# Another order at the seam between two matmul stages: tile 7's copy and W's scale ahead of ar's low part and add 2, tile 0's LoRA product inside tile 1, two matmuls of ones for six

## The reference

```python
def fake_quant(x, scale, zp):
    return (jnp.clip(jnp.round(x / scale + zp), 0, 255) - zp) * scale

x = x + matmul(fake_quant(layernorm(x)), fake_quant(ctx))      # per batch, 512 rows each
y = layernorm(x)
probs = softmax(y @ W_router.T)                                 # 8 experts
topk_p, topk_i = top_k(probs, 2);  topk_p /= sum(topk_p)
combine = sum(one_hot(topk_i, 8) * topk_p)
h = einsum('nd,erd->ner', y, A_stack) * combine                 # rank 16 per expert
out = x + y @ W_base.T + b_base + einsum('ner,eor->no', h, B_stack) * 2.0
```

## Time and profile before

| | |
|---|---|
| median of 3 runs | 176.6 us (176.6 to 176.65) |
| the profiled execution | 176.58 us |
| its span, first to last instruction | 174.8 us |
| TensorE busy | 164.2 us, 94% |
| VectorE busy | 117.9 us, 67% |
| ScalarE busy | 73.9 us, 42% |
| GpSimd busy | 59.8 us, 34% |
| mean granted TensorE clock | 0.998 |

### The profile page before, as it was taken

How to read it: one execution, slowest core, us unless ns; L and a number is a source line. 1 busy time by engine, 2 the same in 40 slices (tenths; PEclk the granted TensorE clock), 3 DMA queues, 4 the chain that set the end, 5 groups by cost and what they waited for, 6 DMA issues and landing times.

```text
span 174.8 us, 2640 instructions
## 1 busy us (share of the span) xinstructions
PE 164.2 (94%) x970; PEld 89.2 (51%) x970; DVE 117.9 (67%) x276; ACT 73.9 (42%) x100; POOL 59.8 (34%) x140
## 2 busy tenths in 40 slices
PE   6988889899989898999999999999999999999992
PEld 3542435345535373645565565564664555556541
DVE  7993749999989999997459238518707906624812
ACT  3096519799978976124252033205205205200000
POOL 8905476888820000583630720540310130000000
PEclk9999999999999999999999999999999999999999
DMA  5999999999910000002002003001100200200211
GB/s 105 375 417 410 410 409 406 411 407 412 401 57 2 0 4 0 0 0 120 4 2 120 0 0 121 3 0 55 68 0 0 120 0 4 120 0 0 120 62 60
DMA packets 6780, 22.74 MB, mean 130 GB/s; under 512 B 880, under 2 KB 1136, under 8 KB 6768
## 3 DMA queue, kind: packets, MB, share of 16 engines
q1 hardware_dynamic: 6624, 22.58, 33.2%
q10 hardware_dynamic: 144, 0.00, 0.0%
HBM read 18.38 MB, written 4.19 MB: 129 GB/s over the span
## 4 chain that ended last, share of the span: by engine, by line
PE 73%; DVE 15%; issue 3%; POOL 3%; ACT 3%; DVEq 0%; ACTq 0%; POOLq 0%
PE ps L805 43%; PE ps L765 10%; PE ps L795 6%; PE ps L774 4%; PE ps L756 2%; DVE xs L519 2%; PE ps L788 2%; PE ps L786 2%; PE ps L787 2%; ACT w_hi L357 2%; DVE w_lo L584 2%; DVE ident L660 2%; PE ps L750 1%; DVE bnx L450 1%; DVE bnx L448 1%
## 5 line engine op out<-in xcount | busy, mean ns | idle before, releaser
L805 PE MATMUL ps<-w_hi,yt_hi 128*128 128x512 f16 x128 | 39.5, 380 | 1.7 <-DVE w_lo L584 1.1
L805 PE MATMUL ps<-w_lo,yt_hi 128*128 128x512 f16 x128 | 39.4, 379 | 0.0
L805 PE MATMUL ps<-w_hi,yt_lo 128*128 128x512 f16 x128 | 39.4, 379 | 0.0
L765 PE MATMUL ps<-a,a_t 128*128 128x512 f16 x128 | 31.2, 379 | 1.9 <-DVE a_t L512 1.1
L318 ACT ACTIVATE a<-stage,prm,inv_s 128x1024 uint8<-128x1024 f32 x16 | 19.5, 1240 | 10.1 <-POOL a L232 6.1
L384 ACT ACTIVATE gate<-gate,ar_undo 128x1 f32<-128x1 f32 x8 | 2.4, 295 | 48.5 <-DVE gate L613 48.5
L612 DVE MAX8 top<-ps 128x8 f32<-128x8 f32 x8 | 1.4, 173 | 31.0 <-PE ps L788 31.0
L805 PEld LDWEIGHTS ps<-w_hi,yt_lo 128*128 128x128 f16 x128 | 12.5, 98 | 15.1
L805 PEld LDWEIGHTS ps<-w_lo,yt_hi 128*128 128x128 f16 x128 | 12.5, 98 | 14.8
L765 PEld LDWEIGHTS ps<-a,a_t 128*128 128x128 f16 x128 | 11.9, 98 | 15.8 <-DVE a_t L512 2.6
L237 POOL TENSOR_TENSOR xs<-xs,corr 128x1024 f32<-128x1024 f32 x5 | 11.8, 2359 | 22.2 <-DVE b_lo L590 22.2
(11 more groups left out here) (133 smaller groups left out, 277.2 us busy)
## 6 DMA issues: line engine op xcount, KB each, us to landing
stage<-in_ctx_kv SPq DMA_DIRECT2D x16, 512.0 KB, 13.4
stage<-in_w_t SPq DMA_DIRECT2D x8, 512.0 KB, 10.6
xs<-in_x SPq DMA_DIRECT2D x7, 512.0 KB, 13.6
out_dram<-xs SPq DMA_DIRECT2D x7, 512.0 KB, 2.7
ar_raw<-in_ar_t SPq DMA_DIRECT2D x1, 544.0 KB, 15.6
xs<-in_x SPq DMA_DIRECT2D x2, 256.0 KB, 3.9
b_raw<-in_b_t SPq DMA_DIRECT2D x1, 512.0 KB, 11.3
bias_sb<-in_bias SPq DMA_DIRECT2D x1, 512.0 KB, 12.0
```

Source lines behind the costliest of these rows:

```text
L765: last = nc.tensor.matmul(ps[:, s1_bank(t) + h, :], a1_t[:, t % 4, k, :], a2[:, n, h * H:(h + 1) * H], start=k == 0, stop=k == K - 1)
L805: ins = nc.tensor.matmul(ps[:, OUT_BANK[p] + h, :], part, rhs[:, k, h * H:(h + 1) * H], start=k == 0 and part is hi and rhs is w_hi, stop= ...
```

## The change

On VectorE add 2 leaves its place ahead of `sum_x1(5)` and goes behind `split_b`; `take_a1t(7)` goes ahead of `peaks_w`; ar's low part goes from behind `scale_w` to between splits 2 and 3; `split_yt(1)` goes ahead of `split_hct(0)`. On TensorE four of six matmuls of ones are gone; `narrow(0)` stands behind `wide(0, 4)` instead of `wide(0, 3)`, with `transpose_y(1)` now ahead of it; `transpose_hc(0)` stands behind `wide(0, 6)` instead of `wide(0, 5)`; `lora(0)`, which ended tile 0, stands behind `wide(1, 0)`, and `narrow(1)` gets a wait for hct's low part, as it writes the bank from which that part is read; `transpose_hc(1)` stands behind k = 4 instead of k = 2. On ScalarE `sum_row(t + 1)` goes behind the two splits that follow it.

```diff
--- before.py
+++ after.py
@@ -423,10 +423,10 @@
                 gate_weight(t)
                 if t + 1 < T:
                     make_y(t + 1)
-                    sum_row(t + 1)
                 split_hct(t)
                 if t + 1 < T:
                     split_yt(t + 1)
+                    sum_row(t + 1)
 
         @block.vector
         def _(dve):
@@ -694,17 +694,16 @@
             sum_x1(4)
             take_a1t(6)
             scale_ar()
-            add_corr(2)
             sum_x1(5)
+            take_a1t(7)
             peaks_w()
-            take_a1t(7)
             scale_w()
-            split_ar()
             sum_x1(6)
             split_w(0)
             split_first_yt()
             split_w(1)
             split_w(2)
+            split_ar()
             split_w(3)
             sum_x1(7)
             dve.wait_ge(iota_ready, 1)
@@ -715,9 +714,10 @@
             gate_tile(0)
             split_w(6)
             split_w(7)
+            split_yt(1)
             split_hct(0)
             split_b()
-            split_yt(1)
+            add_corr(2)
             statistics_y(2)
             add_bias(0)
             for t in range(1, T):
@@ -864,7 +864,7 @@
                     if t + 1 < T and k == 4:
                         transpose_a1(t + 1)
 
-            keep_busy(6, 5)
+            keep_busy(2, 5)
             pe.wait_ge(x1_summed, T - 1)
             pe.wait_ge(first_half_lo, 1)
             for k in range(K):
@@ -873,25 +873,27 @@
                 pe.wait_ge(w_lo_ready, k + 1)
                 wide(0, k, False)
                 if k == 3:
+                    transpose_y(1)
+                if k == 4:
                     pe.wait_ge(x1_summed, T)
-                    pe.wait_ge(yt_lo_ready, 1)
                     pe.wait_ge(ar_lo_ready, 2)
                     narrow(0)
-                if k == 3:
-                    transpose_y(1)
-                if k == 5:
+                if k == 6:
                     transpose_hc(0)
-            pe.wait_ge(b_lo_ready, 1)
-            lora(0, stop=True)
 
             for t in range(1, T - 1):
                 pe.wait_ge(yt_lo_ready, t + 1)
+                if t == 1:
+                    pe.wait_ge(hct_lo_ready, 1)
                 narrow(t)
                 if t >= 2:
                     pe.wait_ge(out_summed, t - 1)
                 for k in range(K):
                     wide(t, k, k == K - 1)
-                    if k == 2:
+                    if t == 1 and k == 0:
+                        pe.wait_ge(b_lo_ready, 1)
+                        lora(0, stop=True)
+                    if k == (4 if t == 1 else 2):
                         transpose_hc(t)
                     if k == (5 if t == 1 else 3):
                         transpose_y(t + 1)
```

## The result

The median of the changed kernel is **178.95 us** (177.86 to 179.52, 4 runs) against 176.6 us (176.56 to 176.65, 4 runs); the ratio is 1.0125 with a 95% interval of 1.007 to 1.0181. The direction was forecast, the size was not: 177.6 was foretold with a range up to 178.4.

The account below looks back on a forecast made before the run. TensorE's start of `wide(0, 6)` at 69.01 us was taken to set the time; +0.93 us from the late gate and +0.11 from the transpose of hc gave +1.04, so 177.6 us, range 177.0 to 178.4.

Parts of the forecast that it names:

- The bound: TensorE is never idle after `wide(0, 6)` starts at 69.01 us, so that start sets the time.
- Part 1: Tile 7's copy and W's scale go ahead of add 2 on VectorE; peak matmul L848 starts 0.94 us earlier, at 50.25.
- Part 2: ar's low part behind split 2 on VectorE: split 3 at 59.42 us, set by ScalarE's high part, all 0.94 earlier.
- Part 3: Four fewer matmuls of ones on TensorE: `wide(0, 0)` 2.3 us earlier at about 55.0, a gain that later waits take back.
- Part 4: `narrow(0)` behind `wide(0, 4)`: gate starts 0.93 us later at 66.14, `wide(0, 6)` 0.93 later at 69.94.
- rival A: The early start is kept, the gate is not late, and the end comes 0.94 us earlier at 175.7; chance 0.05.
- Part 5: Transpose of hc behind `wide(0, 6)` on TensorE costs 0.11 us; tile 0's LoRA product only changes places, +0.
- Part 6: Add 2 put later on VectorE costs nothing: y 2 done at about 81.3 us, its transposes due at 83.5, slack 2.2.
- Sum: Late `wide(0, 6)` +0.93 and transpose of hc +0.11 give +1.04 us, so 177.6 us.
- rival C: TensorE's clock falls in the new hole of some 2.7 us, costing 1 to 2.6 us: 178.6 to 180.2; chance 0.08.
- the granted clock shows less than 1.00 between 65 and 80 us: Sign in TensorE's clock around the new hole before `wide(0, 6)` that would show the forecast wrong.

Follow-up runs that it names:

- experiment 5: The changed kernel with six matmuls of ones again instead of two: median 179.53 us, best run 177.87.
- experiment 3: The changed kernel with `narrow(0)` back behind `wide(0, 3)`, ahead of `transpose_y(1)`: 175.78 us, ratio 0.9954 to the kernel before.
- experiment 4: The kernel before with only `narrow(0)` moved, behind `transpose_y(1)` and `wide(0, 4)`: median 179.89 us, three runs at 178.58 to 178.62, three at 181.17 to 181.19.
- experiment 9: The changed kernel's VectorE and ScalarE orders with TensorE's whole order from the kernel before: 177.05 us, ratio 1.0025.
- experiment 7: The changed kernel with `transpose_hc(0)` back ahead of `wide(0, 6)`: median 179.37 us, two runs at 177.75 and 177.78.
- experiment 2: The changed kernel with 14 matmuls of ones put into TensorE's hole behind `wide(0, 5)`: median 177.82 us, one of six runs at 179.62.
- experiment 6: The changed kernel with `narrow(0)` one block later still, behind `wide(0, 5)`: median 181.93 us.

## Why the prediction was right and wrong

**The bound** was read rightly: TensorE never waits after `wide(0, 6)` in the kernel before, and each shift of that point in the profiles came out at the end.

**Part 1**: L848 at 50.37 (50.25 foretold). The copy started at 49.12 and the peaks were done at 49.97 + 0.26 = 50.23; L848 came 0.14 us after that and not 0.06. In the code TensorE's wait for tile 7's copy stands ahead of L848 itself, and not only of tile 7's product, so L848 needs copy and peaks both; before, the copy ended last of the two (51.13), and that is why moving both ahead gained the time.

**Part 2**: split 3 at 59.53 (59.42), ended by the high part as foretold; split 5 done at 64.48 (64.35). **Part 3**: `wide(0, 0)` at 55.13 (55.0), with the gain spent in the holes ahead of `wide(0, 1)` (0.29 us) and `wide(0, 3)` (1.24); experiment 5 confirms that the ones are free.

**Part 4**, the term that decides, had the right mechanism and about the right size: gate at 66.40 (66.14), VectorE idle 1.93 us (1.8), hole 2.62 (2.7), `wide(0, 6)` 1.21 us later than before (0.93). The 0.28 us more grew in steps, 0.12 at L848, 0.21 at `wide(0, 4)` (63.42 for 63.21), 0.26 at the gate: handovers that took 0.10 to 0.14 us where 0.04 to 0.06 was put. Experiments 3 and 4 undo it and do it alone, for 2.0 us each. (The work that rival A counts as 2.0 us, eight transposes and a `wide`, adds up to 0.87 + 1.29 = 2.16 by part 4's own figures.)

**Part 5**: +0.11 as foretold (71.52 to 71.63), and `narrow(1)` at 72.93 without a wait. "The LoRA product only changes places, +0" is right as a sum and wrong as a reading: experiment 9 shows that the move saves 1.1 us, which y's low part ahead of b's would otherwise have cost.

**Part 6**: no cost, but the slack was less. Statistics of y 2 ended at 76.44 (76.05) and y 2 started at 81.06 where 80.1 was due, since GpSimd's add 3 took 3.30 us (73.91 to 77.21) instead of 2.39, and GpSimd made y 2's scale behind it (see below). The transposes started at 83.63, 1.3 us after y 2 was done and not 2.2.

**Sum**: 177.6 foretold, 177.86 measured in the run that kept its clock. So for that run the mechanism was right and the number was no luck: the start of `wide(0, 6)` moved by 1.21 us and the transpose of hc added 0.11, 1.32 us of the 1.3 measured.

**The step that failed is the chance of rival C**, the fall of the clock, a term that the sum put at nothing and the range left out. The prediction had the hole at 2.7 us, had seen in the earlier trace rows that 2.6 us without work on TensorE were followed by a drop, and had the price at 1 to 2.6 us. It then gave C 0.08, because the hole "lies between busy ones". The runs show the reverse: the clock was lost in 8 of 10 runs, at a price of 0.6 to 1.7 us (2.6 in experiment 4), and that puts the median to 178.95, above the range. That the neighbours of the hole are busy was no protection: in experiment 5 the drop came 1.0 us after TensorE had taken up dense work again, and even a transpose in the middle (experiment 7) did not prevent it. Of the signs that the prediction named, "the granted clock shows less than 1.00 between 65 and 80 us" did not appear in the profile of the changed kernel, which is of a run that kept its clock; it stands in those of experiments 5 and 7. Rival A was out; it is what experiment 3 gives once part 4 is undone.

## What to carry to other kernels

When the product for a side path (here a gate) is moved back behind main-path work, count what is queued behind the side path's engine: here the main path came back for W's low part 6 two blocks later and found it 2.0 us late, nearly the whole 2.16 us of the work put ahead. Weigh each hole that a new order makes in TensorE by its length: in these kernels holes of 1.24 us and less never cost the clock (one unexplained run of experiment 2 apart), holes of 1.43 and 0.86 us with a short transpose between them cost it in 7 of 12 runs, one of 2.6 us in 13 of 16, and one of 3.9 us in all five; nothing between was tried. The price was 0.5 to 2.9 us from run to run, mostly 1.7 and more, and so of the size of what the late start cost by itself (1.3 to 2.0 us). One profile may be of a run that kept its clock, so read the mean clock of every run beside its time, and try filling the hole with idle matmuls; if the median falls and the work behind the hole starts when it did, it was the clock.

## What the runs showed of the hardware that I had not expected

The clock can fall after the idle time is over: in experiment 5 it was granted in full through 2.6 us of idleness and dropped 1.0 us into dense work, then read 0.50 for 3.3 us; in experiment 6, with 3.92 us of idleness, it dropped within the hole. And the same hole costs different amounts from run to run (178.42 and 179.54 us of one kernel on one chip).

The time of GpSimd's add 3 (128x1024) depends on what VectorE does beside it. It took 3.26 to 3.30 us in the ten profiles with VectorE's new order, where it starts beside add 2, and 2.38 to 2.39 us in the two with the old order (the kernel before and experiment 4), where y's low part (L606) stands in the place of add 2; the statistics of y 2 follow in both. That add 2 is the cause follows from this order and was not tried alone. The kernel before and the changed one:

```profile
71.57 2.39 POOL L237 TENSOR_TENSOR xs<-xs,corr 128x1024 f32<-128x1024 f32 x1 [22.22 <-DVE b_lo L590]
...
73.91 3.30 POOL L237 TENSOR_TENSOR xs<-xs,corr 128x1024 f32<-128x1024 f32 x1 [25.40 <-DVE b_lo L590]
77.29 1.09 POOL L248 TENSOR_SCALAR root<-mvy 128x1 f32<-128x1 f32 x1
```

The small operation behind it took 1.09 us for 0.23 before, beside VectorE's `add_bias` (L641, 76.69 to 78.28). Before, the next one (L249) was the slow one beside the same L641, at 1.49 us for 0.58 now, so the small operations cost y 2 nothing more; the add did.
